# A gated recurrence on one core: a block's output and new y made in halves over four steps, a projection's store moved behind z's total

## What is computed

```python
# layer 0: a Haar transform whose coefficients are all scaled by one gate per feature, and its inverse;
# so it is v + v * gate, and with the residual x + x + x * gate = x * (2 + gate)
h = silu(q_pool @ W1.T + b1); gate = sigmoid(h @ W2.T + b2)
x = x + L0(x)
# layer 1: a GRU over the 2048 time steps
z  = sigmoid(x_t @ W_z + h @ U_z + cond @ C_z + b_z)
r  = sigmoid(x_t @ W_r + h @ U_r + cond @ C_r + b_r)
hh = tanh(x_t @ W + (r * h) @ U + cond @ C + b)
h  = (1 - z) * h + z * hh
out = x + h          # for each time step
```

## Time and profile before

| | |
|---|---|
| median of 3 runs | 6800.1 us (6799.94 to 6800.25) |
| profiled execution | 6811.76 us, of which span 6809.9 us |
| granted TensorE clock, mean over the span | 0.996 |
| TensorE matmul / weight load busy | 88% / 83% |
| VectorE busy | 73%, 43503 instructions |
| ScalarE busy | 49%, 22603 instructions |
| chain that ended last | TensorE 71%, VectorE 26%, issue 3% |

### The profile page before, as it was taken

How to read it: one execution, slowest core, us unless ns; L and a number is a source line. 1 busy time by engine, 2 the same in 40 slices (tenths; PEclk the granted TensorE clock), 3 DMA queues, 4 the chain that set the end, 5 groups by cost and what they waited for, 6 DMA issues and landing times.

```text
span 6809.9 us, 488240 instructions
## 1 busy us (share of the span) xinstructions
PE 5998.4 (88%) x200232; PEld 5642.2 (83%) x200232; DVE 4955.6 (73%) x43503; ACT 3331.6 (49%) x22603; POOL 3.5 (0%) x13
## 2 busy tenths in 40 slices
PE   7888888888888888888888888888888888888888
PEld 7888888888888888888888888888888888888888
DVE  5777777777777777777777777777777777777777
ACT  3444444444444444444444444444444444444444
POOL 0000000000000000000000000000000000000000
PEclk8999999999999999999999999999999999999999
DMA  2000000000000000000000000000000000000000
GB/s 84 17 18 15 18 17 18 17 17 17 18 17 18 15 18 17 18 18 15 18 17 18 17 18 15 18 17 18 17 17 17 18 17 18 15 18 18 17 18 15
DMA packets 80315, 129.97 MB, mean 19 GB/s; under 512 B 12336, under 2 KB 18480, under 8 KB 80304
## 3 DMA queue, kind: packets, MB, share of 16 engines
q1 hardware_dynamic: 80304, 129.81, 5.5%
HBM read 20.46 MB, written 8.65 MB: 4 GB/s over the span
## 4 chain that ended last, share of the span: by engine, by line
PE 71%; DVE 26%; issue 3%; SPq 0%; DMA 0%; ACT 0%; ACTq 0%; DVEq 0%
PE pair_r L252 30%; PE ps_z L252 24%; PE pair_h L252 17%; DVE pair_h L487 8%; DVE h_part L522 5%; DVE h_part L541 4%; DVE h_part L527 2%; DVE keep L523 2%; DVE zn L536 2%; DVE h_part L532 2%; PE ps_z L212 0%; DMA u_raw<-in_L_cond_U 0%; PE ps_o L212 0%; DVE u_max L424 0%; PE ps_x L224 0%
## 5 line engine op out<-in xcount | busy, mean ns | idle before, releaser
L252 PEld LDWEIGHTS pair_r<-h_part,u_part 128*128 128x128 f16 x65536 | 1845.1, 96 | 1119.9 <-DVE h_part L541 1115.8
L252 PE MATMUL pair_r<-h_part,u_part 128*128 128x32 f16 x65536 | 2048.7, 177 | 771.1 <-DVE h_part L541 758.6
L252 PE MATMUL pair_h<-rh_part,u_part 128*128 128x32 f16 x65536 | 2016.6, 177 | 12.5 <-DVE rh_part L505 12.5
L252 PE MATMUL ps_z<-h_part,u_part 128*128 128x32 f16 x65536 | 1961.5, 176 | 0.0
L252 PEld LDWEIGHTS pair_h<-rh_part,u_part 128*128 128x128 f16 x65536 | 1842.8, 96 | 17.3 <-DVE rh_part L505 15.7
L252 PEld LDWEIGHTS ps_z<-h_part,u_part 128*128 128x128 f16 x65536 | 1795.3, 95 | 0.0
L487 DVE TENSOR_REDUCE pair_r<-pair_r 128x4 f32<-128x20 f32 x4096 | 759.4, 186 | 818.1 <-PE pair_r L252 615.1
L351 ACT ACTIVATE pair_r<-pair_r 128x4 f32<-128x4 f32 x4096 | 644.8, 158 | 1445.1 <-DVE pair_r L487 1182.4
L487 DVE TENSOR_REDUCE pair_h<-pair_h 128x4 f32<-128x12 f32 x4096 | 717.7, 175 | 665.7 <-PE pair_h L252 665.7
L351 ACT ACTIVATE th_z<-ps_z 128x8 f32<-128x8 f32 x2048 | 364.1, 178 | 1046.0 <-DVE ps_z L487 1046.0
L337 ACT ACTIVATE pair_h<-xp 128x8 f32 (+1 forms) x2049 | 369.9, 181 | 807.8 <-DVE zn L536 807.8
(11 more groups left out here) (70 smaller groups left out, 3275.9 us busy)
## 6 DMA issues: line engine op xcount, KB each, us to landing
w_stage<-w_in SPq DMA_DIRECT2D x384, 256.0 KB, 2.3
x_tok<-in_x SPq DMA_DIRECT2D x68, 128.0 KB, 2.6
out_dram<-o_tok SPq DMA_DIRECT2D x66, 128.0 KB, 2.3
mlp_w<-in_L_cond_W SPq DMA_DIRECT2D x2, 1024.0 KB, 6.9
u_raw<-in_L_cond_U_r SPq DMA_DIRECT2D x1, 1024.0 KB, 5.6
u_raw<-in_L_cond_U_z SPq DMA_DIRECT2D x1, 1024.0 KB, 7.6
u_raw<-in_L_cond_U SPq DMA_DIRECT2D x1, 1024.0 KB, 10.3
w_in<-in_L_cond_W_r SPq DMA_DIRECT2D x4, 256.0 KB, 9.8
```

What stands on the lines that cost most here:

```text
L252: last = nc.tensor.matmul(bank[:, SLOT * m:SLOT * m + WIDE].rearrange("p (r n) -> p r n", n=n), u_part[:, g, part, k, gm * P:(gm + 1) * P] ...
```

## The change

Five things, all in the queues of TensorE, ScalarE, VectorE and in one layout; SP's queue is as it was.
- The history `hist` is laid out with time innermost, so that VectorE reads it contiguously and ScalarE writes its 8 values at a distance.
- `make_out` works on one half of the features: the first behind turn step 0, the second behind turn step 1. TensorE's `put_out` goes from turn step 1 to turn step 2.
- ScalarE copies y_cur in halves in turn steps 1 and 2, and its `put_out` goes from turn step 2 to turn step 3.
- `make_y` works on halves, behind turn steps 2 and 3; counts of `y_ok`, `y_copied` and `o_sum` are doubled.
- `store_projection` goes into body step 4, between z's total and h's first total, and no longer waits for `proj_mm` (z's product of that step stands behind the projection on TensorE).

```diff
--- before.py
+++ after.py
@@ -80,7 +80,7 @@
         y_next = sb("y_next", [P, S, TB])
         y_cur = sb("y_cur", [P, S, TB])
         xp = sb("xp", [P, GM, 2 * TB, B])
-        hist = sb("hist", [P, 2 * TB, S])
+        hist = sb("hist", [P, S, 2 * TB])
         oT = sb("oT", [P, S, TB])
         o_tok = sb("o_tok", [P, D])
         h_cur = sb("h_cur", [P, S])
@@ -177,7 +177,7 @@
                                     base=0, pattern=[[-1, P]], channel_multiplier=1).then_inc(s["ident_ok"], 1)
 
             nc.gpsimd.memset(h_cur[:, :], 0.0)
-            nc.gpsimd.memset(hist[:, TB:2 * TB, :], 0.0)
+            nc.gpsimd.memset(hist[:, :, TB:2 * TB], 0.0)
             nc.gpsimd.memset(y_cur[:, :, :], 0.0)
             nc.gpsimd.memset(h_part[:, 0:HC], 0.0).then_inc(s["hs0"], 1)
             nc.gpsimd.memset(h_part[:, HC:K], 0.0).then_inc(s["hs1"], 1)
@@ -227,7 +227,7 @@
 
 
             pe.wait_ge(s["w_ok"], G)
-            pe.wait_ge(s["y_ok"], 1)
+            pe.wait_ge(s["y_ok"], 2)
             pe.wait_ge(s["gate_ok"], 1)
             for g, bank in enumerate((ps_x, ps_o, ps_p)):
                 for m in range(K):
@@ -301,18 +301,18 @@
                     if turn is not None and u == 0:
                         pe.wait_ge(s["x_in"], turn[0])
                         transpose_block(ps_x, lambda c: x_tok[:, c * P:(c + 1) * P]).then_inc(s["x_tr"], 1)
-                    if turn is not None and u == 1:
+                    if turn is not None and u == 2:
                         put_out(turn[1])
 
             def put_out(nb):
-                pe.wait_ge(s["o_sum"], nb)
+                pe.wait_ge(s["o_sum"], nb * 2 if isinstance(nb, int) else pe.snap(nb * 2))
                 transpose_block(ps_o, lambda c: oT[:, c * B:(c + 1) * B, :].rearrange("p b t -> p (b t)"))\
                     .then_inc(s["o_tr"], 1)
 
             with nc.Fori(0, NB, engines=[mybir.EngineType.PE], hint_back_edge=True) as n:
                 nb = pe.snap(n + 1)
                 steps(pe.snap(n * TB), TURN, turn=(pe.snap(n * BYTES + 2 * BYTES), nb))
-                y_count = pe.snap(n + 2)
+                y_count = pe.snap(n * 2 + 4)
                 with pe.Fori(0, GM) as i:
                     steps(pe.snap(n * TB + i * BODY + TURN), BODY, proj=(pe.snap((n * GM + i + 1) * 16), y_count))
             put_out(NB + 1)
@@ -360,7 +360,7 @@
                     for hf in range(2):
                         tanh(ps_r[hf][:, TANH:TANH + HS], ps_r[hf], R, HS, f"r{hf}_sum", t1, f"r{hf}_th")
 
-                    A(hist[:, prv, :], h_cur[:, :], ACT.Copy)
+                    A(hist[:, :, bass.ds(prv, 1)], h_cur[:, :].unsqueeze(2), ACT.Copy)
                     tanh(th_z[:, :], ps_z, Z, S, "z_sum", t1, "z_th")
 
                     seed(pair_r, R, nxt)
@@ -372,10 +372,10 @@
                     tanh(ps_h[1][:, TANH:TANH + HS], ps_h[1], H, HS, "h1_sum", t1, "h1_th")
                     act.wait_ge(s["zn1"], t1)
                     seed(pair_h, H, nxt)
-                    if turn is not None and u == 1:
-                        act.wait_ge(s["o_sum"], turn)
-                        A(y_cur[:, :, :], y_next[:, :, :], ACT.Copy).then_inc(s["y_copied"], 1)
-                    if turn is not None and u == 2:
+                    if turn is not None and u in (1, 2):
+                        act.wait_ge(s["o_sum"], act.snap(turn * 2 + (u - 2)))
+                        A(y_cur[:, half[u - 1], :], y_next[:, half[u - 1], :], ACT.Copy).then_inc(s["y_copied"], 1)
+                    if turn is not None and u == 3:
                         put_out(turn)
 
             def put_out(nb):
@@ -388,7 +388,7 @@
                 with act.Fori(0, GM) as i:
                     steps(act.snap(n * TB + i * BODY + TURN), BODY, act.snap((n % 2) * TB + i * BODY + TURN))
             act.wait_ge(s["h_ok"], T)
-            A(hist[:, (T - 1) % (2 * TB), :], h_cur[:, :], ACT.Copy).then_inc(s["copied"], 1)
+            A(hist[:, :, (T - 1) % (2 * TB)], h_cur[:, :], ACT.Copy).then_inc(s["copied"], 1)
             put_out(NB + 1)
 
         @block.vector
@@ -449,13 +449,15 @@
             mlp_layer(1)
             dve.wait_ge(s["gate_ok"], 1)
 
-            def make_y(nb):
-
+            def make_y(part, nb, n=None):
                 dve.wait_ge(s["x_tr"], nb)
-                V.tensor_tensor(y_next[:, :, :], ps_x[:, :].rearrange("p (c t) -> p c t", t=TB),
-                                gate2[:, :].unsqueeze(2).broadcast_to([P, S, TB]), ALU.mult).then_inc(s["y_ok"], 1)
-
-            make_y(1)
+                if n is not None:
+                    dve.wait_ge(s["y_copied"], dve.snap(n * 2 + (part + 1)))
+                V.tensor_tensor(y_next[:, half[part], :], ps_x[:, :].rearrange("p (c t) -> p c t", t=TB)[:, half[part], :],
+                                gate2[:, half[part]].unsqueeze(2).broadcast_to([P, HS, TB]), ALU.mult).then_inc(s["y_ok"], 1)
+
+            for part in range(2):
+                make_y(part, 1)
             for g in range(G):
 
                 dve.wait_ge(s["uhi"], g + 1)
@@ -487,7 +489,7 @@
                 return V.tensor_reduce(bank[:, SUM:SUM + m * B].rearrange("p (m b) -> p m b", b=B),
                                        cols(bank, g, 0, m).rearrange("p m a b -> p m b a"), AX_X, ALU.add).then_inc(s[done], 1)
 
-            def step(t1):
+            def step(t1, proj):
                 kc = (slice(0, HC), slice(HC, K))
 
 
@@ -515,6 +517,8 @@
                     gated_low(hf)
                 dve.wait_ge(s["z_mm"], t1)
                 total(ps_z, Z, K, "z_sum")
+                if proj is not None:
+                    store_projection(*proj)
                 dve.wait_ge(s["h0_mm"], t1)
                 total(ps_h[0], H, HC, "h0_sum")
 
@@ -552,40 +556,36 @@
                 new_low(1)
                 V.tensor_tensor(h_cur[:, :], keep[:, :], zn[:, :], ALU.add).then_inc(s["h_ok"], 1)
 
-            def store_projection(count, i, ring):
-
-                dve.wait_ge(s["proj_mm"], count)
+            def store_projection(i, ring):
+
                 V.tensor_tensor(xp[:, i, bass.ds(ring, TB), :].rearrange("p t b -> p b t"),
                                 ps_p[:, 0:P].rearrange("p (b t) -> p b t", t=TB),
                                 v_bias[:, i, :].unsqueeze(2).broadcast_to([P, B, TB]), ALU.add)
 
-            def make_out(ring):
-
-                V.scalar_tensor_tensor(oT[:, :, :], hist[:, bass.ds(ring, TB), :].rearrange("p t c -> p c t"), 1.0 / H_SCALE,
-                                       y_cur[:, :, :], ALU.mult, ALU.add).then_inc(s["o_sum"], 1)
+            def make_out(part, ring):
+
+                V.scalar_tensor_tensor(oT[:, half[part], :], hist[:, half[part], bass.ds(ring, TB)], 1.0 / H_SCALE,
+                                       y_cur[:, half[part], :], ALU.mult, ALU.add).then_inc(s["o_sum"], 1)
 
             def steps(t0, count, proj=None, turn=None):
 
 
                 for u in range(count):
-                    step(dve.snap(t0 + (u + 1)))
-                    if proj is not None and u == K - 1:
-                        store_projection(*proj)
-                    if turn is not None and u == 0:
-
-                        make_out(turn[0])
-                    if turn is not None and u == 2:
-                        dve.wait_ge(s["y_copied"], turn[1])
-                        make_y(turn[2])
+                    step(dve.snap(t0 + (u + 1)), proj if u == K else None)
+                    if turn is not None and u < 2:
+                        make_out(u, turn[0])
+                    if turn is not None and u >= 2:
+                        make_y(u - 2, turn[2], turn[1])
 
             with dve.Fori(0, NB) as n:
                 other = dve.snap(((n + 1) % 2) * TB)
-                steps(dve.snap(n * TB), TURN, turn=(other, dve.snap(n + 1), dve.snap(n + 2)))
+                steps(dve.snap(n * TB), TURN, turn=(other, n, dve.snap(n + 2)))
                 with dve.Fori(0, GM) as i:
 
-                    steps(dve.snap(n * TB + i * BODY + TURN), BODY, proj=(dve.snap(n * GM + i + 2), i, other))
+                    steps(dve.snap(n * TB + i * BODY + TURN), BODY, proj=(i, other))
             dve.wait_ge(s["copied"], 1)
-            make_out((NB - 1) % 2 * TB)
+            for part in range(2):
+                make_out(part, (NB - 1) % 2 * TB)
 
 
 # ---- launch: one core; inputs and outputs as the reference has them ----
```

## The result

The changed kernel takes 6850.6 us (median of 6, 6848.8 to 6852.8) against 6800.5 for the kernel before on the same chip: ratio 1.0073, 95% interval 1.006 to 1.0086, so 50.1 us or 0.7% slower. Its profiled execution lasted 6850.3 us, with a span of 6848.5 and a mean granted clock of 0.985 (0.996 before).

A forecast was written before the change was run, and what follows sets the result against it. Bound by the ring of r product, z product, h product and VectorE's chain to new h; -18.1 - 4.0 - 15.0 + 67.2 + 6.4 - 0.3 = +36.2 us, so 6800.1 becomes 6836.3, range 6818 to 6862.

The forecast's parts named there:

- Output in halves: VectorE's L564: contiguous halves of 0.42 us (0.62 if stride was not the cause) make both steps plain, saving 18.1 us.
- New y in halves: VectorE's L455: a half lasts 0.42 us and hides before r's total, gaining 0.13 per block, 4.0 us.
- Store: VectorE's L558: r's total is freed, at most 0.039 us per store goes, 15.0 us; bounds 0 and 15.0.
- Load behind the output on SP: SP's in-order queue issues w_stage's load after the later output; r product late by 2.1 us per block, 67.2 us.
- Clock: TensorE's pause in each block may lower the granted clock; 0.2 us per block (bounds 0 and 0.5), 6.4 us.
- (a): SP's load of w_stage is not late, so all gains stand: 6763 us; chance 0.06.
- (b): As forecast, but the store delays h's first total and the output half keeps 0.62: 6858 us; chance 0.14.
- (c): Clock falls and stays down for the rest: 184 us on top, 7010 or so; chance 0.02.
- (d): Halves take up what they free, store costs as now, load in time; only output's halves count: 6789 us; chance 0.03.

The follow-up runs named there:

- after_load_first: Changed kernel, but SP issues each block's first w_stage load ahead of the output's wait and two stores; 6768.4 against 6805.9 us for the kernel before, ratio 0.9943.
- after_putout_early: Changed kernel with ScalarE's put_out back at the end of turn step 2, SP's order as changed; 6776.9 against 6805.9 us for the kernel before, ratio 0.9956.
- before_putout_late: Kernel before with only the output's transposes moved to turn step 2 and ScalarE's put_out to turn step 3; 6891.5 against 6805.9 us, ratio 1.0125.

## Why the prediction was right, step by step

Direction, mechanism and place were right, and the time, forecast at 6836, came out 14 us higher, within the range. The range did not hold by luck: the errors of the terms have one sign and do not cancel. The total moved 50.1 us instead of 36.2. The difference from one trace to the other, 6848.5 - 6809.9 = 38.6 us, looks nearer, but by accident: the first profile of before was some 11 us above its median. Medians are compared here.

- **Output in halves, -18.1.** Right: 421 ns a half, both steps plain. The bound of 0.62 for a strided half was right too (616 measured). Its price was not: 0.10 in each of two steps was forecast, 0.10 and 0.05 came, since the second half starts sooner behind h_cur.
- **New y in halves, -4.0.** Right: the steps behind both halves are plain, 3.25 to 3.26.
- **Store, -15.0.** Right (0.083 - 0.045 = 0.038 in 384 steps, 14.5), and for the stated reason: r's total is on time, the store fits ahead of h's first total, and the 0.045 that stay are ScalarE's arithmetic for the wrapped position (3.34, 3.30 and 3.26 in three kernels). It starts 0.33 behind z's total where 0.31 was estimated.
- **Load behind the output on SP, +67.2.** The mechanism is shown by four kernels, the size was low. The projection starts at 5.01 (forecast 4.93). At the full clock r follows 0.32 behind, of which 0.23 was taken from the lower end of the bounds: 5.33 - 3.06 = 2.27 per block instead of 2.1, 5 us in all. And the first block was not thought of: its two stores take 2.14 us to issue and its load 2.8 to land, the pause there is 3.9 long, another 1.4 us.
- **Clock, +6.4.** Too low. The steps of the changed trace give it: the stalled step and the next are 2.64 us longer than two plain ones in the mean of blocks 1 to 31, 0.37 more than the 2.27 above, 12 us. The term allowed up to 0.2 for the projection and took 0.2 for all; where the clock is down in time the projection alone holds r up by 0.26 more (0.58 instead of 0.32), and the lower level lasts up to two steps.
- **Sum of the corrected terms:** 31 x 2.64 + 4.0 - 18.1 - 4.0 - 14.5 = 49, against 50.1 measured.
- **Rivals.** (a) fell: the load was late. But its time, 37 us under before, is what `after_load_first` gave once the load was in time. (b) fell in both its halves. (c) fell: the clock rose again in every block. (d) fell: the halves last 421 ns and the load is late.

## What to carry to other kernels

When a step is moved later, list what stands behind it in every in-order queue that it releases. Here SP, whose code was untouched, carried the whole loss, through a transfer that had nothing to do with the output. A transfer with 0.8 us to spare is one step from the critical path, so issue what can go now ahead of what has to wait for a late result. And where a step is longer than its neighbours, split the excess by the time at which each operation starts: half of what lay behind the store's step was not the store.

## What the runs showed of the hardware

- With a pause of some 2.57 us on TensorE the granted clock went to 1.2 GHz in each of 32 blocks, within the pause or up to 1.6 us behind its end. It cost 0.37 us per block in the steps, most of it in the f32 projection (0.79 instead of 0.47 where the clock was down in time); an f16 product with 32 columns per matmul is hardly slower (1.06 and 1.01 against 1.00 and 0.96).
- A long pause is not needed for it. In `after_putout_early` the clock went to 1.2 GHz in 15 of 32 blocks with no idle of TensorE above 0.68 us, and in `before_putout_late` in 14 blocks ahead of turn step 3, with none above 0.65 in the turn steps. The kernel before, with pauses up to 0.65, kept 2.4 GHz from the second step (78.9 us) to the last. No run here settles what makes the difference.
- Writing out one body of the inner loop on TensorE cost 65 us (115 - 50). TensorE idled inside z's product of turn step 0 with no releaser, and turn steps 0 and 1 lasted 4.57 and 3.43 us in the mean. SP issued the block's load 0.8 us later (3.37 instead of 2.58 behind h_cur of turn step 3). Written out on ScalarE the same kind of edit cost nothing that shows (6748.6). The cause was not settled; no run here tells fetching of instructions from anything else.
- A plain step lasted 3.253 to 3.261 us in the mean in the profiled executions, though the instructions of these steps hardly differ. That is 16 us over 2048 steps, as much as the store's gain. So single executions can't be compared here, only medians of one job, or the excess of a step over its plain neighbours in one trace.
